# Trainium2 kernel: the FFN base product of two token tiles as seven block products

## What is computed

```python
x = x + attn(cond(x, lengths, ...), Wq, Wk, Wv, Wo)
h = einsum('bct,bcd->bdt', x, weights[condition])      # mixes channels of a sequence
xf = h.reshape(-1, 1024)                               # 2048 tokens
probs = softmax(xf @ gate_W.T)                         # 8 experts
w, sel = top_k(probs, 2);  w = w / sum(w)
r = einsum('td,erd->ter', xf, A) * (dense(w, sel)[:, :, None] * 2.0)
x = x + xf @ W_base.T + einsum('ter,eor->to', r, B)    # W_base 1024 x 1024, A 8x8x1024
```

## Time and profile before

| | |
|---|---|
| time, median of 3 runs | 903.14 us (902.97 to 904.03) |
| profiled execution, span from first to last instruction | 900.1 us |
| mean granted TensorE clock | 0.999 |
| PE busy | 876.6 us, 97% |
| weight loads (PEld) | 764.2 us, 85% |
| DVE, ACT, POOL busy | 435.7, 203.0, 399.1 us |
| DMA | 105.36 MB, mean 117 GB/s |

### The profile page before, as it was taken

One profiled execution on the slowest core, in us unless ns is written; L12 is line 12 of the kernel. 1 busy time (PEld: TensorE's weight loads), 2 busy tenths in 40 slices (PEclk: granted clock), 3 DMA queues, 4 the chain that ended last, 5 costly groups with the idle time before them and its releaser, 6 DMA issues.

```text
span 900.1 us, 24902 instructions
## 1 busy us (share of the span) xinstructions
PE 876.6 (97%) x10982; PEld 764.2 (85%) x10982; DVE 435.7 (48%) x931; ACT 203.0 (23%) x369; POOL 399.1 (44%) x310
## 2 busy tenths in 40 slices
PE   3899999999999999999999999999999999999998
PEld 3898999988888888888777777777789999999998
DVE  7455551111222222259887777788524433334444
ACT  4455542100000000023222332233331101011110
POOL 3343664203555556569978888877511000000000
PEclk9999999999999999999999999999999999999999
DMA  3789877211224222156544454544452121222201
GB/s 99 176 207 203 212 179 196 73 58 59 71 72 112 73 71 71 47 182 177 141 141 135 153 156 158 160 150 125 142 190 74 48 95 71 72 72 71 94 25 71
DMA packets 89723, 105.36 MB, mean 117 GB/s; under 512 B 42896, under 2 KB 57616, under 8 KB 89616
## 3 DMA queue, kind: packets, MB, share of 16 engines
q1 hardware_dynamic: 86624, 102.73, 39.2%
q10 hardware_dynamic: 2480, 0.51, 0.3%
q0 software_dynamic: 512, 0.53, 0.2%
HBM read 74.08 MB, written 29.65 MB: 115 GB/s over the span
## 4 chain that ended last, share of the span: by engine, by line
PE 91%; SPq 4%; DMA 3%; DVE 1%; issue 1%; ACT 0%; DVEq 0%
PE ps L939 24%; PE ps L1402 21%; PE ps L1211 20%; PE ps L632 7%; PE ps L903 5%; PE ps L1167 3%; PE ps L1147 3%; SPq L589 3%; PE ps L643 3%; PE ps L1375 2%; DMA toep<-kpad 2%; PE ps L1425 1%; PE ps L1426 1%; SPq L576 1%; DMA kpad<-ksb 1%
## 5 line engine op out<-in xcount | busy, mean ns | idle before, releaser
L1402 PE MATMUL ps<-wb,xf 128*128 128x420 f32 (+1 forms) x1152 | 195.7, 330 | 0.0
L1402 PEld LDWEIGHTS ps<-wb,xf 128*128 128x128 f32 x1152 | 188.3, 188 | 2.9 <-issue 0.2
L939 PE MATMUL ps<-y_hi,w_hi 128*128 128x512 f32 x320 | 125.0, 391 | 0.0
L939 PE MATMUL ps<-y_lo,w_hi 128*128 128x512 f32 x320 | 124.5, 389 | 0.0
L939 PE MATMUL ps<-y_hi,w_lo 128*128 128x512 f32 x320 | 124.5, 389 | 0.0
L1211 PE MATMUL ps<-y_hi 128*128 128x512 f32 x256 | 103.1, 403 | 0.0
L632 PE MATMUL ps<-xc,toep 64*128 64x192 f32 (+4 forms) x1088 | 96.8, 330 | 3.8 <-DMA toep<-kpad 3.8
L1211 PE MATMUL ps<-y_hi,y_lo 128*128 128x512 f32 x256 | 100.0, 390 | 0.0
L1211 PE MATMUL ps<-y_lo,y_hi 128*128 128x512 f32 x256 | 99.9, 390 | 0.0
L632 PEld LDWEIGHTS ps<-xc,toep 64*128 64x128 f32 x1088 | 90.9, 187 | 7.2 <-issue 4.9
L1047 POOL TENSOR_TENSOR rot<-rot,cst 128x512 f32<-128x512 f32 x40 | 52.7, 1319 | 72.9 <-DVE rot L1017 72.9
(11 more groups left out here) (153 smaller groups left out, 1260.2 us busy)
## 6 DMA issues: line engine op xcount, KB each, us to landing
toep<-kpad SPq DMA_DIRECT2D x124, 136.0 KB, 4.0
xc<-in_dram SPq DMA_DIRECT2D x32, 256.0 KB, 4.7
q_rows<-rf SPq DMA_DIRECT2D x32, 256.0 KB, 2.6
q<-q_rows SPq DMA_DIRECT2D x16, 512.0 KB
xr<-in_dram SPq DMA_DIRECT2D x16, 512.0 KB, 4.1
x_scratch<-xr SPq DMA_DIRECT2D x16, 512.0 KB, 2.9
x<-x_scratch SPq DMA_DIRECT2D x16, 512.0 KB, 3.6
out_dram<-x SPq DMA_DIRECT2D x15, 512.0 KB, 2.6
```

The costliest lines, as they stand in the source:

```text
L939: mm = pe.matmul(kq_bank(n), w[a][:, j, :], yt[b][:, j, g * 512:(g + 1) * 512], start=(j == 0 and a + b == 0), stop=(j == NJ - 1 and a == 1))
L1402: mm = pe.matmul(joint_bank(i, piece)[:, 0:hi - lo], xf[i % 2][:, a, t, :], wb[t][:, w4_place(t, c), lo:hi], start=(t == 0 and a + c == 0) ...
```

## The change

The FFN is made for 8 pairs of token tiles (`NP` = 8). Input channels and output columns are cut in halves of 512, and tile 0 and tile 1 of the pair are the two row blocks, so that the base product of a pair is a 2 x 2 by 2 x 2 block product. It is made with seven block products instead of eight (the Winograd form of Strassen's method): x blocks A11, A12 (tile 0), A21, A22 (tile 1), S1 = A21 + A22, S2 = S1 - A11, S3 = A11 - A21, S4 = A12 - S2, and weight blocks with the sums T1 to T4. Each product is 4 blocks of input channels x 3 passes of 512 columns, 12 matmuls; its result is added by DVE to the one or two places of `x1` where it counts, and PSUM banks go on accumulating after such an addition.

- The weight sums T1 to T4 are made in the projections: four rounds (`load_tw`, `combine_tw`, `store_tw`) of a 1 MB load, four DVE subtractions or additions of 512 columns, and a 1 MB store to a new DRAM tensor `t_dram`. The seven weight operands are 14 units of 2 x 512 columns; units 0 to 5 are split at steps 18 to 28, 6 and 7 at the end of attention, 8 to 13 in the first pair.
- ACT copies four mixed blocks from PSUM, DVE makes S1 to S4 (`combine_x`), ACT copies seven high parts, DVE makes the low parts of A11, A12, A22 and POOL those of S1 to S4 (`combined_lo`).
- Gates and ranks are no longer columns of the joint product: `gates_and_ranks` makes them from the operands A11, A12, S1 and A22 with 32 matmuls a pair, 16 of 144 columns (high x high and high x low side by side) and 16 of 72.
- The gate chain handles two tiles at once; the expert product is 4 x 2 matmuls of 512 columns a pair.
- The mixing of tiles 0 and 1 moves ahead of the second to last projection (step `NUNIT`); the others stand after the first three expert products of a pair.
- `bexp_raw` is loaded behind weight units 8 to 13 and the last store, and `ffn_hi` waits for it before units 8 and 9.
- Buffers are laid out anew (`block_at`).

The diff, cut to its core; of the parts from `NP` on only the new lines are shown:

```diff
+        def load_tw(sp, c):
+            if c >= 2:
+                sp.wait_ge(st_tw[c % 2], 16 * (c // 2))
+            sp.dma_start(tw[:, c % 2, :, :].rearrange("p (a n) d -> p a (n d)", a=2), w_ffn[:, c::4, NPROJ:]).then_inc(ld_tw[c % 2], 16)
+        def store_tw(sp, c):
+            sp.wait_ge(v_tw, 4 * c + 4)
+            sp.dma_start(t_dram[:, :, c, :], tw[:, c % 2, :, :]).then_inc(st_tw[c % 2], 16)
+        def combine_tw(v, c):
+            b = [tw[:, c % 2, n, :] for n in range(4)]
+            v.wait_ge(ld_tw[c % 2], 16 * (c // 2 + 1))
+            v.tensor_tensor(b[3], b[3], b[1], ALU.subtract).then_inc(v_tw, 1)
+            v.wait_ge(v_tw, 4 * c + 1)
+            v.tensor_tensor(b[1], b[1], b[0], ALU.subtract).then_inc(v_tw, 1)
+            v.wait_ge(v_tw, 4 * c + 2)
+            v.tensor_tensor(b[0], b[3], b[0], ALU.add).then_inc(v_tw, 1)
+            v.wait_ge(v_tw, 4 * c + 3)
+            v.tensor_tensor(b[2], b[2], b[0], ALU.subtract).then_inc(v_tw, 1)
...
         def qkv_transfers(sp):
             load_weights(sp, 1)
             load_weights(sp, 2)
+            sp.wait_ge(g_ylo, S // 2)
+            load_tw(sp, 0)
+            load_tw(sp, 1)
             for n in range(NVB):
                 sp.wait_ge(v_v, n + 1)
                 g, h = n // NG, n % NG
...
+            for c in range(4):
+                store_tw(sp, c)
+                if c + 2 < 4:
+                    load_tw(sp, c + 2)
...
+                    for ring in range(2):
+                        sp.wait_ge(st_tw[ring], 16 * 2)
...
+                if n in (4, 6):
+                    combine_tw(v, (n - 4) // 2)
             for n in range(4 * NU):
+                if n in (3, 5):
+                    combine_tw(v, (n + 1) // 2)
...
-        W4_TILES = {22: (0,), 24: (1,), 26: (2,), 28: (3,), NUNIT: (4,), NUNIT + 1: (5,)}
+        W4_STEPS = {18 + 2 * u: u for u in range(6)}
+        W4_FIRST = 5
...
-                if 5 <= i < 5 + 2 * WB_FREE:
-                    load_w4(sp, (i - 5) // 2, (W4_HALVES[(i - 5) % 2],))
+                if W4_FIRST <= i < W4_FIRST + 8:
+                    load_w4(sp, i - W4_FIRST)
...
             load_x1(sp, 1)
-            sp.wait_ge(pe_o, NUNIT)
-            for t in range(WB_FREE, WB_EARLY):
-                load_w4(sp, t)
+            sp.dma_start(wg_raw[:, :, 1, :], w_ffn[:, :, 0:NPROJ]).then_inc(ld_wg, 16)
             store_x1(sp, NPAIR - 2)
             sp.wait_ge(pe_y, 2 * NPAIR - 1)
-            load_w4(sp, 6)
-            sp.wait_ge(st_x1[(NPAIR - 2) % 3], 16 * ((NPAIR - 2) // 3 + 1))
-            load_w4(sp, 7)
+            for u in range(8, 14):
+                load_w4(sp, u)
             store_x1(sp, NPAIR - 1)
+            for half in range(2):
+                sp.dma_start(bexp_raw[half * NH:(half + 1) * NH, :], w_b).then_inc(ld_p4, 16)
+            load_x1(sp, 2)
+            load_x1(sp, 3)
...
-                if w == NUNIT + 1:
+                if w == NUNIT:
                     mix_channels(pe, 0)
+                    mix_channels(pe, 1)
...
+                if w in W4_STEPS:
+                    w4_lo(v, W4_STEPS[w])
+                if w == NUNIT:
+                    combine_x(v, 0)
+                    x_lo(v, 0)
+            gate_weights(v)
+            w4_lo(v, 6)
...
+                if w == NUNIT + 1:
+                    combined_lo(gp, 0)
                 if w >= 3:
                     add_residual(gp, (w - 1) // 2 - 1, (w - 1) % 2)
+                if w == NUNIT + 1:
+                    w4_lo(gp, 7)
...
+                    x_hi(act, 0)
+            gate_weights_hi(act)
+            w4_hi(act, 6)
+            w4_hi(act, 7)
...
+        NP = NPAIR // 2
+        A11, S1, S2, S4, S3, A12, A22 = range(NOP)
+        BUILD = (A11, S1, A12, A22, S2, S4, S3)
...
+        def w4_source(u):
+            idx, t = u // 2, slice(u % 2 * 2, u % 2 * 2 + 2)
+            late = slice(4 + t.start, 4 + t.stop)
+            return (w_ffn[:, t, BASE1], t_dram[:, T1_ROW, t, :], t_dram[:, T2_ROW, t, :], w_ffn[:, late, BASE2],
+                    t_dram[:, T3_ROW, t, :], w_ffn[:, late, BASE1], t_dram[:, T4_ROW, t, :])[idx]
+        def load_w4(sp, u):
+            if u >= W4_RING:
+                sp.wait_ge(a_w4, u - W4_RING + 1)
+            sp.dma_start(wb_unit(wb_raw[u]), w4_source(u)).then_inc(ld_w4[u % W4_RING], 16)
+        def w4_hi(act, u):
+            act.wait_ge(ld_w4[u % W4_RING], 16 * (u // W4_RING + 1))
+            if u >= 6:
+                act.wait_ge(pe_y, 2 * NPAIR - 1 if u < 8 else 2 * NPAIR)
+            act.activation(wb_unit(wb_tiles[0][u]), wb_unit(wb_raw[u]), ACT.Copy).then_inc(a_w4, 1)
...
+        def combine_x(v, i):
+            v.wait_ge(a_xraw, 4 * i + 2)
+            v.tensor_tensor(xs(i, S1), xs(i, A22), xs(i, S3), ALU.add).then_inc(v_xs, 1)
+            v.wait_ge(a_xraw, 4 * i + 3)
+            v.wait_ge(v_xs, 4 * i + 1)
+            v.tensor_tensor(xs(i, S3), xs(i, A11), xs(i, S3), ALU.subtract).then_inc(v_xs, 1)
+            v.tensor_tensor(xs(i, S2), xs(i, S1), xs(i, A11), ALU.subtract).then_inc(v_xs, 1)
+            v.wait_ge(a_xraw, 4 * i + 4)
+            v.wait_ge(v_xs, 4 * i + 3)
+            v.tensor_tensor(xs(i, S4), xs(i, A12), xs(i, S2), ALU.subtract).then_inc(v_xs, 1)
+        COMBINED = {S1: 1, S3: 2, S2: 3, S4: 4}
+        def x_hi(act, i):
+            act.wait_ge(pe_mix, 2 * i + 2)
+            if i == 1:
+                act.wait_ge(st_x1[0], 16 * 6)
+                act.wait_ge(g_p4, 1)
+            for op, k, half in ((S3, 1, 0), (A22, 1, 1), (A11, 0, 0), (A12, 0, 1)):
+                act.activation(by_batch(xs(i, op)), mixed(k, half), ACT.Copy).then_inc(a_xraw, 1)
+            for op in BUILD:
+                if op in COMBINED:
+                    act.wait_ge(v_xs, 4 * i + COMBINED[op])
+                else:
+                    act.wait_ge(a_xraw, 4 * i + 4)
+                act.activation(xf(i, op, 0)[:], xs(i, op), ACT.Copy).then_inc(a_xfhi, 1)
...
+        def x_lo(v, i):
+            v.wait_ge(v_xs, 4 * i + 4)
+            for op in (A11, A12, A22):
+                lo(v, i, op).then_inc(v_xflo, 1)
+        def combined_lo(gp, i):
+            for op, used in ((S1, S2), (S2, S4), (S4, S4), (S3, S3)):
+                gp.wait_ge(v_xs, 4 * i + COMBINED[used])
+                lo(gp, i, op).then_inc(g_xflo, 1)
...
+        def sum_bank(i):
+            return bank(4 if i % 2 == 0 else 7)
+        def other_bank(i):
+            return sum_bank(i + 1)
+        D_BANK, C_BANK = bank(5), bank(6)
+        def product(pe, i, idx, dst, start=False):
+            split(pe, i, idx)
+            if i == 0:
+                w4_split(pe, idx)
+            for t in range(4):
                 for a, c in PASSES:
+                    mm = pe.matmul(dst, xf(i, idx, a)[:, t, :], wb(c, idx, t),
+                                   start=(start and t == 0 and a + c == 0), stop=(t == 3 and a == 1),
+                                   skip_group_check=not start)
+            mm.then_inc(pe_p, 1)
+        gate_bank = bank(0)[:, 0:4 * NPROJ].rearrange("p (k c) -> p k c", k=2)
+        def gates_and_ranks(pe, i):
+            for op in (A11, A12, S1, A22):
+                split(pe, i, op)
+            pe.wait_ge(v_xs, 4 * i + 4)
+            if i == 0:
+                pe.wait_ge(v_wg, 2)
+            for k, parts in enumerate((((A11, wg, 0), (A12, wg, 4)), ((S1, wg, 0), (A22, wd, 0)))):
+                for op, w, first in parts:
+                    for t in range(4):
+                        pe.matmul(gate_bank[:, k, :], xf(i, op, 0)[:, t, :], w[:, first + t, :, :].rearrange("p a n -> p (a n)"),
+                                  start=(op in (A11, S1) and t == 0), stop=False)
+                        mm = pe.matmul(gate_bank[:, k, 0:NPROJ], xf(i, op, 1)[:, t, :], w[:, first + t, 0, :],
+                                       start=False, stop=(op in (A12, A22) and t == 3))
+            mm.then_inc(pe_g, 1)
...
         def ffn_matmuls(pe):
+            for i in range(NP):
+                added(pe, 8 * (i - 1) + 5)
+                product(pe, i, 0, sum_bank(i), start=True)
+                gates_and_ranks(pe, i)
+                added(pe, 8 * (i - 1) + 6)
+                product(pe, i, 1, D_BANK, start=True)
+                added(pe, 8 * i + 1)
+                product(pe, i, 2, sum_bank(i))
+                added(pe, 8 * i + 2)
+                product(pe, i, 3, D_BANK)
+                turn_h(pe, i)
+                added(pe, 8 * i + 3)
+                product(pe, i, 4, sum_bank(i))
+                if i == 0:
+                    pe.wait_ge(a_pr, 2 * NPAIR)
                     pe.wait_ge(a_p4, 1)
                     pe.wait_ge(g_p4, 1)
+                pe.wait_ge(a_hthi, i + 1)
+                pe.wait_ge(v_htlo, i + 1)
+                experts(pe, 0, 0, C_BANK, start=True)
+                experts(pe, 0, 1, D_BANK, start=False)
+                experts(pe, 1, 1, other_bank(i), start=True).then_inc(pe_x, 1)
+                if i + 1 < NP:
```

(55 more changed lines are left out.)

442 lines of the change are left out of this document (188 added, 254 removed).

## The result

The changed kernel takes 911.62 us (median of 4 runs, 911.1 to 914.2) against 903.59 us (902.97 to 905.24) before: ratio 1.0102, 95% interval 1.0079 to 1.0124. It is 1.0% slower; the prediction said 1.2% faster, with 885.5 to 898.5 us as its range. The profiled execution has a span of 909.3 us and a mean granted clock of 0.987.

What follows compares the result with a forecast made beforehand. The prediction took PE's own time to bound the kernel: span 900.1 us, less 14.7 saved on PE, plus 4.3 of first-pair stall, is 889.7; with 3.0 from span to median, 892.7 us. The range was 885.5 to 898.5 us.

Steps and rivals of the forecast that it cites:

- The product: FFN on PE: seven products of 12 matmuls a pair take 19.04 us, where the joint product took 24.08.
- Gates and ranks: FFN on PE: 32 narrow matmuls a pair at the observed spacing of 0.11 us, 3.52 us a pair.
- Experts, transposes, mixing: FFN on PE, per pair: experts 1.81 us, two transposes 0.40, mixing 2.18; a whole pair 26.95, against 28.78 before.
- narrow matmuls at their columns: Rival for the FFN's gates: priced by columns, 1.86 us a pair, 13.3 us less, 879.4 us; cheaper gates had chance 0.08.
- serial loads: Rival for the FFN's gates: each weight load costs its whole 0.188 us, 912.7 us; chance 0.06 with other slower ways.
- The projections: Projections: queued stores leave 0.4 us to spare before the third weight block; stall taken as 0, other bound 3 us.
- The steady pairs: FFN pairs 1 to 7: copies, sums and low parts finish before PE needs them; no stall taken.
- 0.62 to 0.85 for 512: Steady FFN pairs: time in us of a 512-column DVE subtraction in SBUF, from 1.29 to 1.81 for 1096 columns.
- The first pair: First FFN pair: PE stalls as `bexp_raw` lands late and DVE's work queues behind; 4.3 us, bounds 2 and 7.
- late operands in each pair: Rival for the FFN pairs: DVE and POOL slow each other, 1.3 us over a pair, 901.8 us; chance 0.08.
- The sum: Whole kernel: 900.1 - 14.7 + 4.3 = 889.7 us of span, with 3.0 us to the median 892.7 us.
- A clock below 1.00 after the first pair's gap: FFN: listed among the signs that would show the forecast wrong, with no size.

Runs made afterwards that it cites:

- gates_no_low: Changed kernel with all low parts on DVE, `bexp_raw` wait moved to the copy reading it, and a pair's 16 gate matmuls of 72 columns left out: 877.19 us.

## Why the prediction was wrong

**The product, Gates and ranks, Experts, transposes, mixing** held. Without stall a pair takes 26.98 us, where I had 26.95; two gate matmuls together take 0.21 us (738.39, 738.60) and each is worth 0.114 us by gates_no_low. The saving on PE was there as forecast, and so the rivals of narrow matmuls at their columns and of serial loads were both wrong. The latter gives 912.7 us, next to the measured time, for a cause that isn't there.

**The projections and Attention** held: PE ran without a gap through the projections, and the third weight block's low part was done at 251.7, 0.9 us before PE needed it.

**The steady pairs** failed, at the step "0.62 to 0.85 for 512". I scaled the shortest and longest duration of L1471 by columns (1.29 gives 0.60, not 0.62; that is of no weight). But the extra time of the longest (1.81 against 1.29) isn't proportional to columns: it is a hold, as long as what POOL still has to run. The trace of the kernel before shows it, in lines that the prediction does not use. DVE's 1.81 us begin 0.6 us before an instruction of POOL ends, and POOL's next one takes 2.96 us, where L1252 takes 1.90 by the median:

```profile
605.73 1.81 DVE L1471 TENSOR_TENSOR wb<-wb_raw,wb 128x1096 fp32r<-128x1096 f32 x1
...
606.34 2.96 POOL L1252 TENSOR_TENSOR sc<-sc,stat 128x1024 f32<-128x1024 f32 x1
```

POOL's 512-column operation lasts 1.29 us, and so DVE's took 1.77 us each, not 0.62 to 0.85. The same sentence placed POOL's low parts behind DVE's ("are then made"), while POOL began at 732.42, before DVE's first. The low part of A11 came just in time (734.7 against 734.9); A12 and A22 were late for the gates, which I had dismissed with "the gates come 2.7 us later". The rival "late operands in each pair" named the mechanism, at 1.3 us a pair; it was 0.85. It had the wrong place, though: A11 at the pair's start, which was not late. I gave it 0.08, and "the longest of eight rows is 0.85" was the wrong evidence against it.

**The first pair** failed in size, by 9.2 us. `bexp_raw` landed at 678.6, where I took 677.4 (1.2 us), and PE had reached the FFN 1.5 us earlier than forecast, so it waited 2.7 us longer for the load. POOL, whose residual the store ahead of that load waits for, was itself held: its four low parts took 6.86 us, where I had 5.2, and its weight unit beside them 3.04, where I had 2.4. The gate chain's halves were to take 3 and 2 us and took 3.3 (681.42 to 684.70) and 7.3 (685.21 to 692.5); with the addition between them 11.0 us where I had 5.65: 5.3 us, by the hold. I had taken their price from the earlier trace rows, where POOL was idle, and the change queues three POOL instructions of 2.4 us beside them. The remaining 1.2 us are about the price of the clock of 0.50 from 694.4 to 697.9 (1.7, half of that stretch).

**The sum** had no term for the clock. That is 6.4 us in the steady pairs and 1 to 2 in the first. "A clock below 1.00 after the first pair's gap" stood among the signs of a wrong forecast, without a price and without a chance. And a small gap in each pair, which the sum would have counted at its length, costs more than its length.

So the sign was lost to two mechanisms that work together: the hold makes gaps, and the gaps bring the clock down. With POOL out of the low parts and the wait moved (label both) the time is 888.26 us, within the range. No part of the range allowed for both mechanisms.

## What to carry to other kernels

Work moved from DVE to POOL "in parallel" is no gain when both work in SBUF: the two streams took as long as one after the other (6.85 and 7.0 us), and the tiny operations of a latency chain waited for POOL's whole instruction. Price a DVE operation by what POOL runs beside it after the change, and measure a new chain from rows where POOL is as busy as it will be. A gap of 1 us on PE is not priced at 1 us: ask what the clock does after it (a fall cost 1.6 to 4.8 us here).
